# GpSimd's order in the first chunk of a recommendation tower: layer 1's low parts before chunk 3's gathers, and twelve idle-time matmuls instead of fourteen

## The chip, the cores and the metric

The kernel runs on one core of a Trainium2 chip. The metric is device time in microseconds (us). Times of runs and of the profiled execution are given apart, since the profile describes one execution alone. PE is TensorE, DVE VectorE, ACT ScalarE, POOL GpSimd, and SP the engine that issues most of the transfers.

## The reference

For each of 512 samples, 39 embedding rows of 16 numbers are gathered from 39 tables. A three-layer compressed interaction network follows, and then a small dense network:

```python
e = stack([tbl_f[ids[:, f]] for f in range(39)], axis=1)        # (512, 39, 16)
x0 = xk = e
for idx, (W, b) in enumerate([(w0, b0), (w1, b1), (w2, b2)]):   # 128 outputs each
    z = relu(einsum('bhd,bkd,hks->bsd', x0, xk, W) + b[None, :, None])
    if idx != 2:
        xk = z[:, :64, :]; direct.append(z[:, 64:, :])
    else:
        direct.append(z)
logit = sum(concatenate(direct, axis=1), axis=-1)               # (512, 256)
h = concatenate([logit, dense_ctx], axis=1)
y = relu(relu(h @ W_top1 + b_top1) @ W_top2 + b_top2) @ W_top3
```

## The kernel before, in words

The batch is cut into 16 chunks of 32 samples, and a chunk's 32 samples times 16 dimensions are the 512 columns of every large operand. For each chunk GpSimd gathers the embedding rows with ten indirect transfers into `emb` (line 360), PE transposes them in two pieces (lines 739 and 744), ACT copies the pieces into `xt`, and SP writes them to the scratch `fields` in memory and loads them back in two layouts: `rep` and `rot` for layer 0 (rotated rows), `bc` for layers 1 and 2 (lines 290, 295, 308 and 315). Even chunks use one buffer of `emb` and `bc`, odd chunks the other.

Each layer then multiplies pairs of rows elementwise on DVE and feeds the products to PE, which sums them over the weights into `z`. The products come in groups of two tiles, of three kinds. A group of kind `w` goes to PE whole, in float32 (DVE line 677, PE line 763). A group of kind `v` or `g` is split: ACT makes the high part (line 496), the low part is raw minus high, and PE runs three matmuls for each tile (lines 753 to 755). For kind `v` DVE computes the low part (line 645), for kind `g` GpSimd does (line 371, `low_g`). Layers 1 and 2 have three `g` groups each, called here the first, second and third low part of a layer and chunk, and a half tile whose low part GpSimd makes partly, too (`stack`, line 365). In layer 1 PE takes the groups in the order 0, 2, 1, 3, 4, 5, 6, 9, 7, 8, where 3, 6 and 8 are of kind `g`; in layer 2 it takes the groups 1, 0, 2, 4, 3, 5 and then 8, 9, 7, 6, where 2, 5 and 6 are of kind `g`.

Every engine runs its own list, in the order written, and semaphores hold the engines together. PE, DVE and ACT go through the layers and chunks in this order: layer 0 of chunk 0, layer 1 of chunk 0, layer 0 of chunk 1, layer 2 of chunk 0, layer 0 of chunk 2, layer 1 of chunk 1, and then three steps for each later phase. GpSimd's list is written out by hand: 30 gathers of chunks 0 to 2, and then chunk 3's ten gathers mixed with the low parts of layers 1 and 2 of chunk 0. A low part waits for its high part, a gather of chunk 3 for the transposes of chunk 1. DVE has two raw slots for `g` products, so its third product of a layer waits for GpSimd's first low part; ACT's high part of the third waits until PE has used the first. When layer 1's last matmul on `z` is done, ACT writes `xk`, with which DVE can begin layer 2 of the chunk.

Ahead of layer 0 of chunk 0, PE has nothing to do until the first products are there, and `keep_busy` runs `FIRST_ROWS` matmuls whose result nobody reads (line 776). A matmul in float32 shows as two rows in the profile.

Of the kernel before, what the change touches and what calls it, by code (L numbers as in the profile page):

```python
# [13 lines left out]
GATHERS = -(-FIELDS // BY)  # L14
# [38 lines left out]
SECTIONS = T1 // SECTION  # L53
STORES = 2 * BY
FOLDS = 3
FIRST_ROWS, FIRST_KEPT = 14, 2
H1, H2, DENSE = 512, 256, 16

DENSE_AT = (0, 32, 64)
# [20 lines left out]
def tower(nc, A, fields, out):  # L80
# [4 lines left out]
    with ExitStack() as ctx:  # L85
# [259 lines left out]
        def _(pool):  # L345
# [9 lines left out]
            def gather(c, columns=range(GATHERS)):  # L355
                if c >= 2:
                    pool.wait_ge(transposed, 2 * (c - 1))
                for j in columns:
                    landed = gathered_first if c == 0 and j < PART // DIM else gathered[c % 2]
                    pool.indirect_dma_start(emb[c % 2][:, j * DIM:(j + 1) * DIM], None, A["tables"],  # L360
                                            bass.IndirectOffsetOnAxis(rows_all[:, c, j:j + 1], 0)).then_inc(landed, 16)
# [5 lines left out]
            def low_part(layer, c, i):  # L367

                k, m = NO["g"][layer, c, groups_of(layer, "g")[i]], ROWS[layer]
                pool.wait_ge(high_ready["g"], k + 1)  # L370
                pool.tensor_tensor(low["g"][0:m, k % PART_SLOTS["g"]], raw[0:m, k % RAW_SLOTS], high["g"][0:m, k % PART_SLOTS["g"]], ALU.subtract).then_inc(low_ready["g"], 1)  # L371
# [20 lines left out]

            for c in range(3):
                gather(c)
            gather(3, range(0, 4))
            low_part(1, 0, 0)
            gather(3, range(4, 6))
            low_part(1, 0, 1)
            stack_part(1, 0)
            low_part(1, 0, 2)  # L400
            gather(3, range(6, 8))
            low_part(2, 0, 0)
            gather(3, range(8, GATHERS))
            low_part(2, 0, 1)
            low_part(2, 0, 2)
            fold01(0)
# [494 lines left out]
```

## Time and profile before

| | us |
|---|---|
| median of 3 runs | 637.71 (637.43 to 641.0) |
| profiled execution, its time | 639.57 |
| profiled execution, its span | 637.2 |
| mean granted clock of TensorE, as a share | 0.995 |

The span runs from the first to the last instruction of the profiled execution; 2.37 us of that execution's time lie around it. The times in rows are counted from the span's start. PE is busy for 606.0 us of the span (95%), DVE for 567.8 (89%), POOL for 485.0 (76%) and ACT for 331.1 (52%).

### The profile page before, as it was taken

The numbers are of one execution on the slowest core, as the hardware profiler recorded it, in microseconds if no ns is written. First come the engines' busy times: TensorE is split into PE (matmuls) and PEld (weight loads), VectorE is DVE, ScalarE is ACT, GpSimd is POOL, SyncE is SP. The second block draws the span as 40 slices with busy tenths as digits, with TensorE's granted clock in tenths as the row PEclk, the third lists the DMA queues.
The fourth block names the chain that finished last, engine by engine and source line by source line (L and its number), as shares of the span: only waits on it lengthen the run. The fifth ranks groups of instructions, "written<-read, shape, count | busy, mean of one in ns | idle before, by whom it ended". The sixth has DMA issues, their size and how long they took to land.

```text
span 637.2 us, 6536 instructions
## 1 busy us (share of the span) xinstructions
PE 606.0 (95%) x2044; PEld 379.8 (60%) x2044; DVE 567.8 (89%) x534; ACT 331.1 (52%) x411; POOL 485.0 (76%) x424
## 2 busy tenths in 40 slices
PE   0896999999999999999999999999999999999998
PEld 0344656565666566666666566666656665756563
DVE  0368799999999999999999999999999999989850
ACT  1323636554747464655646464655547473645432
POOL 6878568987888888888888888888888664565740
PEclk9997999999999999999999999999999999999999
DMA  9799579793948577693939585785939494350200
GB/s 197 179 314 343 177 218 347 217 362 72 351 104 296 177 244 239 180 310 97 366 66 346 132 285 184 224 267 157 332 74 343 101 314 147 129 200 1 72 1 0
DMA packets 126048, 130.13 MB, mean 204 GB/s; under 512 B 60990, under 2 KB 67662, under 8 KB 126015
## 3 DMA queue, kind: packets, MB, share of 16 engines
q1 hardware_dynamic: 117391, 128.27, 63.1%
q0 software_dynamic: 5120, 1.32, 2.0%
q10 hardware_dynamic: 3504, 0.14, 0.4%
q8 instruction: 16, 0.26, 0.2%
q14 instruction: 17, 0.14, 0.1%
HBM read 123.31 MB, written 6.39 MB: 204 GB/s over the span
## 4 chain that ended last, share of the span: by engine, by line
PE 81%; POOL 9%; DVE 5%; issue 3%; DMA 1%; ACT 1%; ACTq 0%; DVEq 0%
PE z L763 35%; PE z L753 14%; PE z L755 13%; PE z L754 13%; POOL emb L360 7%; POOL low_g L371 2%; DVE whole L677 2%; DVE low_v L645 1%; PE z L841 1%; PE z L770 1%; PE z L771 1%; DVE raw L670 1%; DVE raw_bank L664 1%; DMA emb<-in_tables,ids_all 1%; PE raw_bank L831 1%
## 5 line engine op out<-in xcount | busy, mean ns | idle before, releaser
L371 POOL TENSOR_TENSOR low_g<-raw,high_g 128x1024 fp32r<-128x1024 f32 x96 | 229.2, 2390 | 72.8 <-ACT high_g L496 72.4
L763 PE MATMUL z<-whole,w 128*128 128x512 f32 (+2 forms) x608 | 282.1, 593 | 1.8 <-DVE whole L677 1.0
L360 POOL DMA_INDIRECT emb<-in_tables,ids_all x160 | 157.6, 985 | 35.6 <-issue 28.2
L763 PEld LDWEIGHTS z<-whole,w 128*128 128x128 f32 (+2 forms) x608 | 112.9, 189 | 99.9 <-issue 84.4
L496 ACT ACTIVATE high_v<-raw_bank 128x1024 fp32r<-128x1024 f32 (+1 forms) x112 | 114.6, 1023 | 92.8 <-DVE raw_bank L664 92.0
L677 DVE TENSOR_TENSOR whole<-bc,xk 128x1024 f32<-128x1024 f32 (+1 forms) x128 | 137.9, 1078 | 7.9 <-ACT xk L507 5.4
L496 ACT ACTIVATE high_g<-raw 128x1024 fp32r<-128x1024 f32 x96 | 101.5, 1057 | 78.6 <-DVE raw L670 60.1
L645 DVE TENSOR_TENSOR low_v<-raw_bank,high_v 128x1024 fp32r<-128x1024 f32 (+1 forms) x112 | 136.2, 1216 | 3.8 <-ACT high_v L496 3.8
L753 PE MATMUL z<-high_v,w_high 128*128 128x512 f32 (+1 forms) x224 | 126.3, 564 | 1.3 <-DVE low_v L645 1.3
L664 DVE TENSOR_TENSOR raw_bank<-bc,xk 128x1024 f32<-128x1024 f32 x96 | 117.6, 1225 | 7.4 <-ACT xk L507 4.6
L670 DVE TENSOR_TENSOR raw<-bc,xk 128x1024 f32<-128x1024 f32 x96 | 116.3, 1212 | 0.5 <-POOL low_g L371 0.5
L753 PE MATMUL z<-high_g,w_high 128*128 128x512 f32 x192 | 82.6, 430 | 7.2 <-POOL low_g L371 7.1
L755 PE MATMUL z<-low_v,w_high 128*128 128x512 f32 (+1 forms) x224 | 88.0, 393 | 0.0
L754 PE MATMUL z<-high_v,w_low 128*128 128x512 f32 (+1 forms) x224 | 87.6, 391 | 0.0
L755 PE MATMUL z<-low_g,w_high 128*128 128x512 f32 x192 | 75.8, 395 | 0.0
L754 PE MATMUL z<-high_g,w_low 128*128 128x512 f32 x192 | 75.4, 393 | 0.0
L753 PEld LDWEIGHTS z<-high_v,w_high 128*128 128x128 f32 (+1 forms) x224 | 42.4, 189 | 31.4 <-issue 22.3
L754 PEld LDWEIGHTS z<-high_v,w_low 128*128 128x128 f32 (+1 forms) x224 | 42.4, 189 | 27.9 <-issue 22.3
L507 ACT ACTIVATE xk<-z,bias 64x512 f32<-64x512 f32 x64 | 41.6, 650 | 31.5 <-DVE whole L677 17.8
L753 PEld LDWEIGHTS z<-high_g,w_high 128*128 128x128 f32 x192 | 36.3, 189 | 20.6 <-POOL low_g L371 10.1
L755 PEld LDWEIGHTS z<-low_v,w_high 128*128 128x128 f32 (+1 forms) x224 | 42.2, 188 | 9.8
L677 DVE TENSOR_TENSOR whole<-rot,left 120x1024 f32<-120x1024 f32 (+1 forms) x45 | 45.2, 1031 | 0.0
(70 smaller groups left out, 407.3 us busy)
## 6 DMA issues: line engine op xcount, KB each, us to landing
bc<-fields SPq DMA_DIRECT2D x64, 1024.0 KB, 7.3
rot<-fields SPq DMA_DIRECT2D x32, 512.0 KB, 4.8
rot<-fields SPq DMA_DIRECT2D x16, 768.0 KB, 7.0
bc<-fields SPq DMA_DIRECT2D x16, 768.0 KB, 5.2
fields<-xt SPq DMA_DIRECT2D x64, 80.0 KB
bc<-fields SPq DMA_DIRECT2D x32, 128.0 KB, 6.1
rep<-fields SPq DMA_DIRECT2D x48, 80.0 KB
emb<-in_tables,ids_all POOLq DMA_INDIRECT x160, 4.9
```

The costliest lines, as they stand in the source:

```text
L360: pool.indirect_dma_start(emb[c % 2][:, j * DIM:(j + 1) * DIM], None, A["tables"], bass.IndirectOffsetOnAxis(rows_all[:, c, j:j + 1], 0)). ...
L371: pool.tensor_tensor(low["g"][0:m, k % PART_SLOTS["g"]], raw[0:m, k % RAW_SLOTS], high["g"][0:m, k % PART_SLOTS["g"]], ALU.subtract).then_ ...
L496: act.activation(high[kind][0:m, k % slots], src, ACT.Copy).then_inc(high_ready[kind], 1)
L507: act.activation(xk[layer][half * KEEP:(half + 1) * KEEP, :], z[layer][0:KEEP, :], RELU, bias=bias[0:KEEP, layer:layer + 1]).then_inc(x_re ...
L645: nc.vector.tensor_tensor(low["v"][0:m, k % slots], raw_bank[0:m], high["v"][0:m, k % slots], ALU.subtract).then_inc(low_ready["v"], 1)
L664: nc.vector.tensor_tensor(raw_bank[0:m], left, right, ALU.mult).then_inc(raw_ready["v"], 1)
L670: nc.vector.tensor_tensor(raw[0:m, k % RAW_SLOTS], left, right, ALU.mult).then_inc(raw_ready["g"], 1)
L677: nc.vector.tensor_tensor(whole[0:rows, n % WHOLE_SLOTS, 0:len(tiles)], left, right, ALU.mult).then_inc(whole_ready, 1)
L753: nc.tensor.matmul(out_z, w_high[0:m, n, :], high[kind][0:m, k % slots, u], start=first, stop=False)
L754: nc.tensor.matmul(out_z, w_low[0:m, n, :], high[kind][0:m, k % slots, u], start=False, stop=False)
L755: ins = nc.tensor.matmul(out_z, w_high[0:m, n, :], low[kind][0:m, k % slots, u], start=False, stop=False)
L763: ins = nc.tensor.matmul(z[layer][:, :], w[layer][0:m, WHOLE_AT[layer, t], :], whole[0:m, k % WHOLE_SLOTS, u], start=(t == GT * TAKEN[laye ...
```

## The change

GpSimd issues none of chunk 3's gathers ahead of the first low part of layer 1 of chunk 0, two between the first and the second, and the other eight behind the third. Layer 2's three low parts of chunk 0 then follow without gathers between them. PE runs twelve matmuls of `keep_busy` in place of fourteen.

```diff
-FIRST_ROWS, FIRST_KEPT = 14, 2
+FIRST_ROWS, FIRST_KEPT = 12, 2
...
             for c in range(3):
                 gather(c)
-            gather(3, range(0, 4))
             low_part(1, 0, 0)
-            gather(3, range(4, 6))
+            gather(3, range(0, 2))
             low_part(1, 0, 1)
             stack_part(1, 0)
             low_part(1, 0, 2)
-            gather(3, range(6, 8))
+            gather(3, range(2, GATHERS))
             low_part(2, 0, 0)
-            gather(3, range(8, GATHERS))
             low_part(2, 0, 1)
             low_part(2, 0, 2)
             fold01(0)
```

On POOL, from its first gather on, this stood in a row (`emb<-in_tables,ids_all` is a gather with its count behind the x, `low_g` a low part, `stack` the half tile's):

```order
L360 DMA emb<-in_tables,ids_all 128x16 x34
L371 TENSOR_TENSOR low_g<-raw,high_g 128x1024
L360 DMA emb<-in_tables,ids_all 128x16 x2
L371 TENSOR_TENSOR low_g<-raw,high_g 128x1024
L365 TENSOR_TENSOR stack<-stack_raw,stack 64x512
L371 TENSOR_TENSOR low_g<-raw,high_g 128x1024
L360 DMA emb<-in_tables,ids_all 128x16 x2
L371 TENSOR_TENSOR low_g<-raw,high_g 128x1024
L360 DMA emb<-in_tables,ids_all 128x16 x2
L371 TENSOR_TENSOR low_g<-raw,high_g 128x1024 x2
```

At the same place on POOL, this stands now:

```order
L360 DMA emb<-in_tables,ids_all 128x16 x30
L371 TENSOR_TENSOR low_g<-raw,high_g 128x1024
L360 DMA emb<-in_tables,ids_all 128x16 x2
L371 TENSOR_TENSOR low_g<-raw,high_g 128x1024
L365 TENSOR_TENSOR stack<-stack_raw,stack 64x512
L371 TENSOR_TENSOR low_g<-raw,high_g 128x1024
L360 DMA emb<-in_tables,ids_all 128x16 x8
L371 TENSOR_TENSOR low_g<-raw,high_g 128x1024 x3
```

The first low part moved ahead of four gathers, and the fourth, layer 2's first, now has all forty gathers of four chunks before it, as against thirty-eight.

On PE, between the transposes of chunk 0 and the first products of layer 0, this stood before:

```order
L739 MATMUL z<-ident,emb 128x128
L744 MATMUL z<-ident,emb 32x128
L776 MATMUL z<-w,ident 128x512 x14
L763 MATMUL z<-whole,w 128x512 x2
L753 MATMUL z<-high_v,w_high 128x512
```

And this stands there now (the lines of the file have moved up by two):

```order
L737 MATMUL z<-ident,emb 128x128
L742 MATMUL z<-ident,emb 32x128
L774 MATMUL z<-w,ident 128x512 x12
L761 MATMUL z<-whole,w 128x512 x2
L751 MATMUL z<-high_v,w_high 128x512
```

Two of the matmuls with `ident` are gone, and nothing else moved on PE.

## Rows read from the trace of the kernel before

**Rows 1.** The page's chain of work that ended last, by engine.
```profile
PE 81%; POOL 9%; DVE 5%; issue 3%; DMA 1%; ACT 1%; ACTq 0%; DVEq 0%
```

**Rows 2.** Stretches: us, busy time (instructions) per engine, clock, DMA share, GB/s.
```profile
106.00:125.00 19.00, 18.71 (x62) 11.49 (x63) 18.46 (x18) 9.98 (x13) 17.22 (x18) 1.00 0.84 251
...
200.00:300.00 100.00, 100.00 (x345) 63.83 (x343) 99.13 (x94) 56.30 (x70) 85.13 (x76) 1.00 0.68 215
```

**Rows 3.** Timeline of PE, end of keep_busy: start, us, what.
```profile
31.64 2.31 PE L776 MATMUL z<-w,ident 128*128 128x512 f32 x5
...
33.79 1.88 PE L763 MATMUL z<-whole,w 120*128 120x512 f32 x4
```

**Rows 4.** Timeline of DVE, ahead of and in layer 0 of chunk 0.
```profile
24.23 3.62 DVE L634 TENSOR_TENSOR w_low<-bc,w_high 128x3328 fp32r<-128x3328 f32 x1 [12.13 <-ACT w_high L550]
...
31.38 1.23 DVE L677 TENSOR_TENSOR whole<-rot,rep 120x1024 f32<-120x1024 f32 x1 [0.45 <-DMA rot<-fields]
```

**Rows 5.** Timeline of POOL: gathers and low parts; brackets hold idle time before.
```profile
24.45 4.21 POOL L360 DMA_INDIRECT emb<-in_tables,ids_all  x1 [0.30 <-issue]
...
45.45 0.94 POOL L360 DMA_INDIRECT emb<-in_tables,ids_all  x1 [0.30 <-issue]
...
50.44 0.94 POOL L360 DMA_INDIRECT emb<-in_tables,ids_all  x1 [0.30 <-issue]
51.41 2.36 POOL L371 TENSOR_TENSOR low_g<-raw,high_g 128x1024 fp32r<-128x1024 f32 x1
...
56.16 2.41 POOL L371 TENSOR_TENSOR low_g<-raw,high_g 128x1024 fp32r<-128x1024 f32 x1
...
59.75 2.39 POOL L371 TENSOR_TENSOR low_g<-raw,high_g 128x1024 fp32r<-128x1024 f32 x1
62.30 0.96 POOL L360 DMA_INDIRECT emb<-in_tables,ids_all  x1 [0.16 <-issue]
...
71.65 2.39 POOL L371 TENSOR_TENSOR low_g<-raw,high_g 128x1024 fp32r<-128x1024 f32 x1 [7.14 <-ACT high_g L496]
```

**Rows 6.** Timeline of PE, from layer 1 of chunk 0 to chunk 4's transposes.
```profile
53.82 0.79 PE L753 MATMUL z<-high_g,w_high 128*128 128x512 f32 x1 [5.34 <-POOL low_g L371]
...
59.58 0.80 PE L753 MATMUL z<-high_g,w_high 128*128 128x512 f32 x1
...
63.61 0.39 PE L753 MATMUL z<-high_g,w_high 128*128 128x512 f32 x1
...
65.21 0.39 PE L771 MATMUL z<-stack,w_low 128*128 128x512 f32 x1
...
74.44 0.39 PE L753 MATMUL z<-high_g,w_high 128*128 128x512 f32 x1
...
106.03 0.51 PE L753 MATMUL z<-high_g,w_high 128*128 128x512 f32 x1 [0.83 <-POOL low_g L371]
...
114.11 0.33 PE L739 MATMUL z<-ident,emb 128*128 128x128 f32 x1 [0.26 <-DMA emb<-in_tables,ids_all]
```

**Rows 7.** Timeline of ACT and DVE around layers 1 and 2 of chunk 0.
```profile
45.67 1.06 ACT L496 ACTIVATE high_g<-raw 128x1024 fp32r<-128x1024 f32 x1 [1.23 <-DVE raw L670]
...
53.87 1.22 DVE L670 TENSOR_TENSOR raw<-bc,xk 128x1024 f32<-128x1024 f32 x1 [0.53 <-POOL low_g L371]
...
67.00 1.23 DVE L664 TENSOR_TENSOR raw_bank<-bc,xk 128x1024 f32<-128x1024 f32 x1 [3.22 <-ACT xk L507]
```

**Rows 8.** Stretches around PE's long wait; columns as in rows 2.
```profile
50.20:50.40 0.20, 0.00 (x0) 0.00 (x0) 0.20 (x2) 0.01 (x1) 0.00 (x0) 1.00 1.11 374
50.40:50.60 0.20, 0.00 (x0) 0.00 (x0) 0.20 (x1) 0.20 (x1) 0.16 (x1) 0.52 1.06 392
...
57.00:58.00 1.00, 1.00 (x5) 0.86 (x4) 0.00 (x0) 0.98 (x2) 1.00 (x1) 0.88 1.10 397
```

**Rows 9.** Issues of `rot` for chunk 1, second and third, and their landing.
```profile
L295 SPq DMA_DIRECT2D rot<-fields x2: 464/466/469, 50.3 to 50.8; - x2
...
DMA to landing us min/median/max: 6.3/7.1/7.9
```

## The prediction, made before the changed kernel ran

> **What bounds the kernel now.** The chain of waits, read first, ends on PE for 81% of the span and on POOL for 9% [rows 1]. A look at stretches says where which of them holds: from 200 to 300 us PE has no idle time at all and runs at the full granted clock [rows 2], so whatever PE gains ahead of that reaches the end, unless something later gives it back. So I looked for PE's idle time in the first 125 us. The largest is in layer 1 of chunk 0: PE waits 5.34 us, until 53.82, for POOL's first low part [rows 6]. That low part starts at 51.41 [rows 5], though its high part was ready at 45.67 + 1.06 = 46.73 [rows 7]: POOL was still issuing gathers. The last of its 34 gathers starts at 50.44, and the thirtieth ends at 45.45 + 0.94 = 46.39 [rows 5]. The wait also has a second price. TensorE's granted clock falls from 1.00 to about half (2.4 to 1.2 GHz) at 50.4, while PE stands still, and is back only within the stretch from 57 to 58 [rows 8], so the first matmuls after the wait run slowly. Two smaller waits of PE follow, 0.83 us at 106.03 and 0.26 us at 114.11, both at work that POOL delivers [rows 6].
>
> **The low parts of layer 1.** Four gathers leave the place ahead of the first low part. From the thirtieth to the thirty-fourth gather it is 50.44 - 45.45 = 4.99 us, 1.25 each [rows 5]. POOL runs without a wait there, so the first low part starts at 51.41 - 5.0 = 46.4, if its high part is there. Before, that was ready at 46.73; the second edit (below) brings it to 45.6. Behind it POOL's list is the same as before up to the third low part (two gathers, low, stack, low), so I shift the rows by 5.0: the second low part goes from 56.16 to 51.2, the third from 59.75 to 54.75, and its end from 62.14 to 57.1 [rows 5].
>
> PE gets its first g group at 48.8 rather than 53.82. The second low part ends at about 53.6. From PE's second g group to its third, 63.61 - 59.58 = 4.0 us pass [rows 6], at the full clock, so the third group comes at 57.6 at the latest, when its low part is 0.5 us old. From there to the end of layer 1 it is 65.21 + 0.23 - 63.61 = 1.83 us (0.23 is the distance of such matmuls at the full clock: 65.21 - 63.61 over seven). Layer 1 of chunk 0 ends at 59.4 instead of 65.44, **6.0 to 6.1 us earlier**: the five of POOL, and about one that PE and DVE lost otherwise (the slow matmuls; and DVE's third raw product, which waited 0.53 us for the same low part [rows 7]). DVE was idle for 3.22 us up to 67.00 for exactly this end [rows 7], by way of ACT, so it starts layer 2 at about 61.
>
> **The eight gathers.** They now stand between layer 1's third low part and layer 2's first. POOL's first gather behind the third low part moves from 62.30 to 57.3 [rows 5]; seven more at 1.25 and the length of one end at 57.3 + 8.75 + 0.95 = 67.0. Layer 2's first low part, from 71.65, could with DVE's new times start at 65.5, so the gathers now hold it up: it goes from 67.05 to 69.4. Before, POOL stood idle for 7.14 us at this place [rows 5], which pays for the gathers. PE, which took that low part at 74.44 [rows 6], gets it at 69.45, **5.0 earlier**, and waits about 1.2 us for it: a new wait, POOL's again. The two low parts behind it have lost the gathers that stood between, so with high parts 6.1 us earlier POOL is 6.1 ahead from the third of them on. Chunk 3's embeddings, whose last gather starts at 66 instead of 75, are not late for anyone.
>
> **The two smaller waits.** With DVE and POOL 6.1 us ahead and PE only 5.0, the wait of 0.83 at 106.03 goes, and that at 114.11 shrinks with it: POOL's order behind layer 2 is unchanged, and chunk 4's last gather is also 6.1 earlier. PE ends up 5.0 + 0.83 + 0.26 = **6.1 us earlier** past 114, where DVE's and POOL's 6.1 are the next limit. Behind that PE is full and keeps it.
>
> **Two matmuls of keep_busy fewer.** The last rows of keep_busy are (33.79 - 31.64) / 5 = 0.43 us apart [rows 3]. Two matmuls are four rows, 1.72 us; PE would be through at 32.07. DVE's first whole product ends at 31.38 + 1.23 = 32.61 [rows 4], so PE starts at 32.65 and 1.14 of the 1.72 is saved; what hid it is gone, DVE is what comes last there. Layer 0 of chunk 0, ACT's `xk` and DVE's products of layer 1 are all 1.14 us earlier. At the end of the kernel it is not added to the 5.0, since POOL's gathers from 3.88 us on don't depend on it: it only sees to it that high parts are ready before POOL wants them. By itself it would be worth 0 to 1.1 us, in this sum 0.3 (46.73 against 46.4).
>
> **What is unknown.** The third part of chunk 1's `rot` is issued at 50.8 and lands 7.9 us later, at 58.7 [rows 9]. DVE's layer 0 of chunk 1 will want it at about 57.4 (the third raw product at 52.2, then four instructions of at most 1.22 each). If SP's chain moves by the same 1.14 us, it lands at 57.6 and nothing is lost; if the transfer engines are so full that it doesn't move (shares of 1.06 to 1.11 in that stretch [rows 8]; these are means that can exceed one), DVE loses 1.3, of which 0.5 is free ahead of layer 2, so 0.8. I take 0.2, nearer to the first, because SP waits there for ACT. A gain below nothing is excluded, since nobody waits for it earlier than this.
>
> **The sum.** 6.1 - 0.2 = 5.9 us. The profiled span would be 631.3, its time 639.57 - 5.9 = 633.7. The profiled execution lies 1.86 above the median of the runs; against the median it is 637.71 - 5.9 = **631.8**. A measurement of this kernel tells about 1% (6.4 us) from no change, and the forecast lies just inside it.
>
> **Rival: the clock falls all the same.** The gap of 5.34 becomes one of 53.82 - 48.8 = 5.0 less, plus the 1.1 by which PE is there earlier, so some 1.5 us; then PE waits briefly again for the second low part. Before, the clock fell about 2 us into PE's wait [rows 6, 8], which speaks against it, but between 47 and 54 PE is still idle for over a quarter of the time (1.5, then some 0.4 ahead of the next two groups). Then some fourteen matmuls cost 0.2 us more each (0.43 for 0.23), 2.8, of which the gaps absorb 1 or more: the end is 1 to 2 us worse, 632.8 to 633.8. Such a delay reaches the end in full, since it also takes from DVE's and POOL's 6.1.
>
> **Rival: the eight gathers are held up, and the kernel gets slower.** One gather took 4.21 us instead of 0.94, from 24.45 [rows 5], just while DVE ran a long subtraction with both inputs in SBUF, from 24.23 to 27.85 [rows 4]. If the eight gathers met such work, each would cost up to 3.3 more, 26 us in all, and layer 2's first low part would start at 93 instead of 71.65. Slower than before begins at 5.0 us of delay, two gathers blocked. What speaks against it: between 57 and 67 DVE's products take one factor from a PSUM bank, and the gathers from 45.45 to 50.44, beside such products, all kept 0.94. Blocked for four gathers of the eight, it is 8 us slower: 646.
> The Trainium skill says the same of the cause (SBUF — State Buffer, Who interferes with whom): a VectorE instruction with two SBUF inputs contends with a GpSimd instruction that reads SBUF, and the one that comes second blocks fully, while one SBUF input does not contend. By that rule the eight gathers run free, as in the sum; the trace agrees at 4.21 us.
>
> **Rival: the gain is given back.** If chunk 4's embeddings or DVE were the real limit of the stretch up to 125, where DVE is busy for 18.46 of 19.00 us [rows 2], and they didn't move, PE would wait for them and the end stay where it is, at 637. Against it: DVE's wait at 67.00 is for PE's layer 1, which does move, and POOL's idle 7.14 us shows that POOL can.
>
> **How the numbers follow.** Forecast 0.72, with its own range from 631.0 to 632.7 (gains of 6.7 to 5.0: POOL's part alone at the one end, 0.6 of luck with transfers and matmuls at the other). The clock 0.14, given back 0.07, gathers held up 0.04, and 0.03 for a larger gain. The range from 630.9 to 633.9 takes in the forecast and the clock and leaves out the rest. Faster by over 1% needs 6.4 us, which the upper edge of the forecast and the larger gain reach: 0.29. Slower by over 1% is the blocked gathers: 0.03. Within 1%: 0.68.
>
> **What would show it.** POOL's first low part starts at 46.4 and PE's wait ahead of it is 1.5 instead of 5.34; the clock stays at 1.00 through 50 to 58; layer 1 of chunk 0 ends at 59.4; POOL's eight gathers run from 57.3 to 67.0 at 1.25 each; PE waits about 1.2 us for layer 2's first low part, at 69.45; the waits at 106.03 and 114.11 are smaller or gone. The prediction is wrong if DVE starts layer 2 later than 62, if a gather of the eight is much longer than 0.94, or if PE's steady part does not start 5 to 6 us earlier.

## The result, and the profile after

| | before | changed |
|---|---|---|
| median of 5 runs | 637.85 | 635.36 |
| lowest to highest | 637.43 to 641.0 | 634.74 to 635.69 |
| profiled execution, its time | 639.57 | 634.74 |
| profiled execution, its span | 637.2 | 632.4 |

The ratio of the runs is 0.9949, with a 95% interval from 0.9929 to 0.9968. The change is faster, clear of the noise, but by 2.5 us between the medians, where 5.9 were forecast. The two profiled executions are 4.83 us apart, much nearer to the forecast than the medians: the later sections are about this difference.

POOL's timeline in the changed kernel, which answers to rows 5:

```profile
45.00 0.94 POOL L360 DMA_INDIRECT emb<-in_tables,ids_all  x1 [0.30 <-issue]
46.95 2.38 POOL L371 TENSOR_TENSOR low_g<-raw,high_g 128x1024 fp32r<-128x1024 f32 x1 [1.00 <-ACT high_g L494]
...
51.70 2.41 POOL L371 TENSOR_TENSOR low_g<-raw,high_g 128x1024 fp32r<-128x1024 f32 x1
54.55 1.29 POOL L365 TENSOR_TENSOR stack<-stack_raw,stack 64x512 fp32r<-64x512 f32 x1 [0.44 <-ACT stack L501]
55.81 2.38 POOL L371 TENSOR_TENSOR low_g<-raw,high_g 128x1024 fp32r<-128x1024 f32 x1
58.34 0.96 POOL L360 DMA_INDIRECT emb<-in_tables,ids_all  x1 [0.16 <-issue]
...
67.09 0.94 POOL L360 DMA_INDIRECT emb<-in_tables,ids_all  x1 [0.30 <-issue]
68.05 2.40 POOL L371 TENSOR_TENSOR low_g<-raw,high_g 128x1024 fp32r<-128x1024 f32 x1
```

The first low part starts at 46.95 instead of 51.41 [rows 5], and now it is POOL that waits, 1.00 us, for ACT's high part. The eight gathers run unhindered from 58.34 to 68.03, and layer 2's first low part comes right behind them, in the place where POOL stood idle for 7.14 us before [rows 5].

PE's timeline, which answers to rows 6 (the second piece of the same engine is its start of layer 0, as in rows 3):

```profile
49.39 0.51 PE L751 MATMUL z<-high_g,w_high 128*128 128x512 f32 x1 [0.77 <-POOL low_g L371]
51.69 0.51 PE L751 MATMUL z<-high_v,w_high 128*128 128x512 f32 x1 [0.64 <-DVE low_v L643]
...
60.34 0.39 PE L769 MATMUL z<-stack,w_low 128*128 128x512 f32 x1
70.51 0.51 PE L751 MATMUL z<-high_g,w_high 128*128 128x512 f32 x1 [0.76 <-POOL low_g L371]
109.28 0.33 PE L737 MATMUL z<-ident,emb 128*128 128x128 f32 x1 [0.22 <-DMA emb<-in_tables,ids_all]
```

```profile
20.69 13.40 PE L774 MATMUL z<-w,ident 128*128 128x512 f32 x24 [0.36 <-ACT xt L478]
33.93 1.88 PE L761 MATMUL z<-whole,w 120*128 120x512 f32 x4
```

PE's wait of 5.34 us is down to 0.77, layer 1 of chunk 0 ends at 60.6 instead of 65.4, and the transposes of chunk 4 start at 109.28 instead of 114.11, 4.83 earlier, which is the whole difference of the two executions. But layer 0 starts at 33.93, where before it started at 33.79 [rows 3], although keep_busy has four rows fewer: its 24 rows took 13.4 us, 0.56 each, because the first of them ran slowly for longer. The granted clock is listed as 1.00 there in both profiles, so what these rows show is the distance of the rows, and not a clock.

DVE's timeline between the two, around the end of chunk 1's layer 0 and the start of chunk 0's layer 2 (67.00 before [rows 7]):

```profile
59.10 1.22 DVE L675 TENSOR_TENSOR whole<-rot,left 120x1024 f32<-120x1024 f32 x1 [0.37 <-DMA rot<-fields]
...
62.13 1.23 DVE L662 TENSOR_TENSOR raw_bank<-bc,xk 128x1024 f32<-128x1024 f32 x1
```

Stretches as in rows 8 and 2: the clock stays at 1.00 through the place where it fell before, and the steady part is as full as it was.

```profile
50.40:50.60 0.20, 0.20 (x2) 0.17 (x1) 0.20 (x2) 0.07 (x1) 0.04 (x1) 1.00 1.05 410
57.00:58.00 1.00, 1.00 (x5) 0.68 (x4) 1.00 (x2) 0.36 (x1) 1.00 (x1) 1.00 1.05 391
200.00:300.00 100.00, 100.00 (x346) 64.18 (x345) 99.10 (x95) 56.77 (x72) 85.05 (x76) 1.00 0.70 214
```

### The profile page after: what moved, and what is told of

Same layout as the page of the kernel before. It is cut to its first block, busy times and chain, and to the rows that moved or that the text cites. A ratio compares the mean times of both kernels' runs of the same rounds, so it can differ in the third digit from the quotient of the medians.

```text
span 632.4 us, 6528 instructions
## 1 busy us (share of the span) xinstructions
PE 604.9 (96%) x2040; PEld 378.5 (60%) x2040; DVE 568.1 (90%) x534; ACT 331.1 (52%) x411; POOL 484.8 (77%) x424
## 3 DMA queue, kind: packets, MB, share of 16 engines
HBM read 123.31 MB, written 6.39 MB: 205 GB/s over the span
## 4 chain that ended last, share of the span: by engine, by line
PE 84%; DVE 6%; POOL 4%; issue 2%; DMA 2%; ACT 1%; ACTq 0%; DVEq 0%
PE z L761 36%; PE z L751 14%; PE z L753 14%; PE z L752 13%; POOL emb L360 2%; PE z L774 2%; DVE whole L675 2%; DVE low_v L643 2%; DMA emb<-in_tables,ids_all 2%; POOL low_g L371 2%; DVE raw L668 1%; DVE raw_bank L662 1%; PE z L839 1%; PE z L768 1%; PE z L769 1%
```

## The experiments

Each is compared with runs of the kernel before on the same chip in the same hour. The medians of those lie between 637.85 and 639.40, so the ratios are compared, and not the times, which the expectations name. For the changed kernel the ratios were 0.9949 and, in a second set, 0.9953. Profiled executions can be compared directly, across chips too: in all sixteen, from the start of chunk 4's transposes (109.28 to 114.11 us) to the end of the execution's time it is 525.42 to 525.48 us. So whatever sets them apart has happened before that point.

**The new order on POOL alone, and the two matmuls alone.**

```diff
 # e1: the changed kernel
-FIRST_ROWS, FIRST_KEPT = 12, 2
+FIRST_ROWS, FIRST_KEPT = 14, 2
 # e2: the kernel before
-FIRST_ROWS, FIRST_KEPT = 14, 2
+FIRST_ROWS, FIRST_KEPT = 12, 2
```

> The new order on POOL with the old fourteen matmuls of keep_busy. Theory 1: the order brings the gain, and in the new order layer 0's end reaches the end of the kernel; how long keep_busy takes depends on when TensorE's clock rises in an execution (23.1 us in the profile of before, 26.7 in that of the changed kernel), and two matmuls more cost 0 to 1.7 us: a median of 635.4 to 637.0, best guess 636.2, that is 0 to 1.7 us over the changed kernel. Rival: the two matmuls are worth nothing or did harm: 635.4 or less.

> The old order on POOL with twelve matmuls of keep_busy. Theory 1: the first low part still starts behind 34 gathers at about 51.4, whatever layer 0 does, so the median stays at that of before, 637.4 to 638.2. Rival: an earlier layer 0 reaches the end by another way (DVE): 636.5 to 637.0.

The order alone: 636.23 (634.87 to 636.97), ratio 0.9964 (0.9950 to 0.9978). The two matmuls alone: 638.73 (637.51 to 640.36) beside 638.42, ratio 1.0002 (0.9990 to 1.0015). So the gain is the order's, and in the old order the two matmuls are worth nothing. The changed kernel's ratios (0.9949 and 0.9953) would put the two matmuls at 0.7 to 1.0 us in the new order, as theory 1 says, but the intervals overlap, and e5 and e6 below speak against it. What e1's expectation calls the rise of the clock, at 23.1 and 26.7 us, is the moment at which keep_busy's rows come closer together.

**The kernel before, twice more.** Nothing is edited in e4 and e11; they show how one execution differs from the next.

> The kernel before, once more, for a second profile and for the width of its times. Theory 1: another execution shows the clock fall and rise at other moments around PE's wait, its time lies nearer to 637.8 than the first profile's 639.57, and the ratio is 1.000 within 0.002. Rival: the fall lies at 50.4 and the rise near 57.4 again, with about the same eight slow matmuls, and the 1.7 us between the first profile and the median lie elsewhere.

> The kernel before, a third profile. Theory: its time goes with two things that differ between executions, the start of POOL's first low part (51.41 at 639.57, 50.54 at 639.31) and the time for which the clock stays at half behind PE's wait (6.83 us in both): an execution near 637.8 shows the low part at 49.5 to 50.5 or a half clock of about 3.4 us. Rival: an execution near 637.8 shows neither.

The runs of the kernel before beside e4 lie between 636.37 and 640.5 (31 runs, median 638.42), and e4's own median is 638.51, ratio 1.0003 (0.9989 to 1.0017). The profile of e4 (639.31) is like the first: PE waits 4.10 us, and the clock is at half until past 57, though it fell 0.7 us later than in the first. So it does not decide between theory 1 and the rival. In the profile of e2 (637.51) PE waits 3.83 us, and the clock is back by 56. PE's timeline and a stretch of e4, and PE's timeline and two stretches of e2:

```profile
52.95 0.79 PE L753 MATMUL z<-high_g,w_high 128*128 128x512 f32 x1 [4.10 <-POOL low_g L371]
```

```profile
57.00:58.00 1.00, 1.00 (x4) 0.81 (x3) 0.31 (x1) 0.64 (x2) 1.00 (x2) 0.55 1.01 356
```

```profile
51.88 0.50 PE L753 MATMUL z<-high_g,w_high 128*128 128x512 f32 x1 [3.83 <-POOL low_g L371]
```

```profile
55.00:56.00 1.00, 1.00 (x4) 0.76 (x4) 1.00 (x2) 0.86 (x1) 1.00 (x1) 0.65 1.04 391
56.00:57.00 1.00, 1.00 (x5) 0.61 (x4) 0.98 (x3) 0.80 (x2) 1.00 (x2) 1.00 1.07 393
```

The profile of e11 (636.60) differs more. POOL's and PE's timelines and a stretch of e11:

```profile
25.20 3.87 POOL L360 DMA_INDIRECT emb<-in_tables,ids_all  x1 [0.31 <-issue]
...
49.56 2.38 POOL L371 TENSOR_TENSOR low_g<-raw,high_g 128x1024 fp32r<-128x1024 f32 x1
```

```profile
35.61 0.59 PE L763 MATMUL z<-whole,w 120*128 120x512 f32 x1
...
51.99 0.50 PE L753 MATMUL z<-high_g,w_high 128*128 128x512 f32 x1 [1.70 <-POOL low_g L371]
```

```profile
52.00:53.00 1.00, 1.00 (x4) 0.85 (x5) 1.00 (x2) 0.79 (x1) 0.90 (x1) 1.00 1.10 334
```

In this execution of the unchanged kernel POOL's first low part starts at 49.56 instead of 51.41 [rows 5]; keep_busy ended late, so layer 0 started at 35.61 instead of 33.79 [rows 3], and PE's wait is 1.70 instead of 5.34 [rows 6]; the clock does not fall at all. It is 2.97 us faster than the first profiled execution, and its chunk 4 transposes start 2.97 us earlier (111.14). The wait that the prediction read from rows 6 is the longest of the four. The execution near 637.8 that the expectation asked for is e2's: its low part starts at 49.45, and its clock is at half for 3.4 us.

How often the clock falls can be counted without profiles, since each run's mean granted clock is on record. It is 0.995 in the first profile and in e4 (6.8 us at half), 0.997 in e2 (3.4 us) and 1.000 in e11. The 77 runs of the kernel before that stand beside the experiments have 0.995 in 32, 0.997 in 40 and 1.000 in 5, and their times go with it:

| mean clock | runs | median, us |
|---|---|---|
| 0.995 | 32 | 639.53 |
| 0.997 | 40 | 638.17 |
| 1.000 | 5 | 636.99 |

So the clock falls in nearly every run of the old order, a run like e11 is rare, and the first profiled execution belongs to the slower of the two common groups. The sets differ in the share of these groups: 3 of 17 runs have 0.995 in the set with the median 638.26, and 9 of 14 in that with 639.40. All eleven runs of the changed kernel have 1.000.

The start of the low part moves because the 34 gathers ahead of it take more or less time: one of them meets DVE's long subtraction and takes 4.21 us [rows 5], 3.31 in e4, 3.50 in e2, and one to three later ones meet DVE's first products. Over the 34 gathers, the time beyond 0.94 each is 5.4 us in the first profile, 4.7 in e4, 3.6 in e11 and 3.5 in e2, and the low parts start at 51.41, 50.54, 49.56 and 49.45.

**PE's wait filled.** Five matmuls that nobody reads, into a bank that is idle there, ahead of layer 1's first g group of chunk 0 in the kernel before. e10 is the same kernel a second time.

```diff
                 for g in TAKEN[layer]:
...
                     else:
+                        if (layer, c, g) == (1, 0, 3):
+                            keep_busy(5, xk[1])
                         split_group(layer, c, g)
```

> The kernel before, with five matmuls that nobody reads (into an idle bank) in PE's 5.3 us wait for the first low part. Theory 1: the half clock behind that wait cost the profiled execution of before about 1.6 us (eight matmuls at 0.43 instead of 0.23), the median execution less; filled, the clock stays at 1.00 through 48 to 58, and the median is 636.9 to 637.7 with a smaller spread than before. Rival a: every execution of before pays the 1.6: 636.2. Rival b: the half clock costs nothing at the end: 637.85.

> The kernel with PE's wait filled, once more, for a second profile (its times fall into two groups, near 636.9 and near 638.4). Theory: the clock stays at 1.00 and the time goes with the start of POOL's first low part (50.1 at 636.90): 638.4 would go with a start near 51.5. Rival: in the slower group the clock falls all the same.

The median is 637.94 beside 638.42, ratio 0.9986 (0.9973 to 0.9998). The profile of e3 (636.90), PE's timeline and a stretch:

```profile
48.58 4.45 PE L776 MATMUL xk<-w,ident 128*128 128x512 f32 x10
...
52.54 0.72 PE L753 MATMUL z<-high_g,w_high 128*128 128x512 f32 x1
```

```profile
57.00:58.00 1.00, 1.00 (x5) 0.60 (x4) 1.00 (x1) 0.00 (x0) 1.00 (x2) 1.00 1.00 369
```

One of e3's twelve runs took 3607 us, for a reason that is not known, and is not in the ratio. The clock stays up, in all twelve runs, and the kernel gains a little, 0.1%: theory 1's size, not the 1.6 us that rival a takes from every execution. The second look refutes what was expected of it. At 638.17 its low part starts at 49.62, not near 51.5; the clock is at 1.00, so the rival is out, too. There keep_busy ended at 35.3, where it ended at 34.0 in e3, the filling ran on to 53.76, past the low part's end at 52.0, and held PE up; DVE also waited 1.26 us for the half tile's transfer. The two starts of layer 0 are 1.29 us apart and the two times 1.27; whether that is what makes the two groups of this kernel's times, two profiles don't show.

Since the filling can hold PE up by itself, e3's median prices the slow clock too low. The profiles give the price more directly: from its first g group to the end of layer 1 PE takes 11.62 us in the first profile, 12.29 in e4 and 11.62 in e2, where the clock is at half for a part of it, and 10.36 in e11 and 10.34 in e3 and e10, where it is not. That is 1.3 to 1.9 us (in e2 with a wait of DVE for `bc` in it, 0.98 us).

**What the end follows in the new order.** e5 is the changed kernel again; e6 and e7 have fewer matmuls of keep_busy; e8 moves the last two gathers.

```diff
 # e6, e7: the changed kernel
-FIRST_ROWS, FIRST_KEPT = 12, 2
+FIRST_ROWS, FIRST_KEPT = 10, 2      (e7: 8)
 # e8: the changed kernel
-            gather(3, range(2, GATHERS))
+            gather(3, range(2, 8))
             low_part(2, 0, 0)
+            gather(3, range(8, GATHERS))
```

> The changed kernel once more, for a second profile and as the mark for the three kernels beside it. Its median is 635.0 to 635.8, and the ratio 0.995 within 0.002.

> The changed kernel with ten matmuls of keep_busy in place of twelve. Theory 1: in the new order the end of layer 0 reaches the end of the kernel, until POOL's thirtieth gather (45.9 to 46.4) comes last; keep_busy ended at 33.9 in the profile of the changed kernel, where DVE's product was ready at 32.3, so four rows of 0.43 fewer save up to 1.7 us there and up to 1.0 at the end: 634.6 to 635.0. Rival: keep_busy's length does not reach the end, 635.4 as before the edit.

> The changed kernel with eight matmuls of keep_busy. Theory 1: nothing is left to save beyond ten, since DVE's product at 32.3 comes last: 634.4 to 635.0, the same as with ten. Rival: PE's idle time ahead of layer 0 (up to 3.7 us) lets the clock fall, layer 0 runs at half speed and ends up to 2 us later: 635.8 to 637.

> The changed kernel with the last two of chunk 3's gathers behind layer 2's first low part instead of ahead of it. That low part can start at 66.7 instead of 68.05, and PE's wait of 0.76 us there goes. Theory 1: what is earlier at the end is set by DVE's chain from layer 1's end (4.8 us earlier than in the profile of before), not by this low part, and PE's gain is taken by its waits near 101 and 109: 635.1 to 635.6, no change. Rival: this low part sets the end: 634.5 to 634.8.

| | median | ratio, 95% interval |
|---|---|---|
| e5, as changed | 635.73 | 0.9953 (0.9940 to 0.9967) |
| e6, ten | 635.65 | 0.9956 (0.9944 to 0.9969) |
| e7, eight | 636.48 | 0.9972 (0.9962 to 0.9982) |
| e8, two gathers later | 635.55 | 0.9957 (0.9944 to 0.9969) |

e8 agrees with theory 1. Its profile shows the low part of layer 2 earlier, and PE's wait for it down to 0.16 us, and what PE gained there it waits at the next two places:

```profile
69.86 0.50 PE L752 MATMUL z<-high_g,w_high 128*128 128x512 f32 x1 [0.16 <-POOL low_g L371]
101.95 0.50 PE L752 MATMUL z<-high_g,w_high 128*128 128x512 f32 x1 [0.88 <-POOL low_g L371]
110.08 0.33 PE L738 MATMUL z<-ident,emb 128*128 128x128 f32 x1 [0.34 <-DMA emb<-in_tables,ids_all]
```

e7 agrees with the rival: PE stood idle for 3.22 us ahead of layer 0 and the clock fell in it, so that layer 0 ran at half. It does so in part of the runs only: the mean clock is 0.995 in five of the twelve (median 637.58), 0.997 in four (636.26) and 1.000 in three (635.66).

```profile
33.00 2.04 PE L761 MATMUL z<-whole,w 120*128 120x512 f32 x2 [3.22 <-DVE whole L675]
```

```profile
34.00:36.00 2.00, 2.00 (x5) 0.97 (x3) 1.88 (x3) 0.00 (x0) 1.70 (x2) 0.50 1.06 379
```

e6 refutes theory 1 on its own ground. Layer 0 did start earlier, at 32.60 instead of 33.93, and yet nothing came of it. PE's, DVE's and SP's timelines in e6:

```profile
32.60 1.96 PE L761 MATMUL z<-whole,w 120*128 120x512 f32 x4 [0.95 <-DVE whole L675]
...
60.69 0.39 PE L769 MATMUL z<-stack,w_low 128*128 128x512 f32 x1
```

```profile
53.14 0.69 DVE L697 TENSOR_TENSOR stack_raw<-bc,xk 128x512 f32<-128x512 f32 x1 [1.49 <-DMA bc<-fields]
```

```profile
41.07 6.39 SPq L256 DMA_DIRECT2D fields<-xt  x8
47.50 0.43 SPq L308 DMA_DIRECT2D bc<-fields  x1
47.98 1.15 SPq L315 DMA_DIRECT2D bc<-fields  x2
```

DVE waits 1.49 us for the transfers of `bc` at the half tile, a wait that is not there in the first profile of either kernel. SP begins chunk 1's stores 1.1 us earlier than before, but issuing the eight takes 6.39 us while the transfers of `bc` ahead of them are still running, and the last part of `bc` is issued at 47.5 and 48.0. An earlier layer 0 does not bring this issue forward: in the first profiles of both kernels, e1, e2, e4, e5, e6 and e8 layer 0 starts between 32.60 (e6) and 34.44 (e1), and the issue stands between 46.89 and 47.95, at 47.50 in e6 and at 47.12 in e1. e5 has the same wait at 0.88 us; e1 and e8 don't have it, and wait for the third part of chunk 1's `rot` instead, 1.04 and 1.24 us. What e6 still has in hand at the start of layer 2 (62.48, where e5 has 62.96) it gives back to the next transfer, chunk 2's `rot`:

```profile
80.29 1.22 DVE L675 TENSOR_TENSOR whole<-rot,left 120x1024 f32<-120x1024 f32 x1 [0.56 <-DMA rot<-fields]
```

In the end chunk 4's transposes start at 110.17 in e1, 110.12 in e5 and 110.19 in e6, with fourteen, twelve and ten matmuls and layer 0 1.84 us apart. So theory 1 became theory 2: the transfers between 42 and 60 us hold DVE's chain.

**The transfers.** e9 (with ten matmuls) loads the half tiles ahead of chunk 1's stores; e13 (twelve) and e14 (ten) load all of chunk 0's `bc` ahead of them.

```diff
 # e9: half_tiles is the loop over half of load_broadcasts, a function of its own, left out there for c = 0
             load_broadcasts(0, range(SECTIONS - 1))
+            half_tiles(0)
             store_issue(1)
             load_broadcasts(0, range(SECTIONS - 1, SECTIONS))
 # e13, e14
-            load_broadcasts(0, range(SECTIONS - 1))
+            load_broadcasts(0)
             store_issue(1)
-            load_broadcasts(0, range(SECTIONS - 1, SECTIONS))
```

> The changed kernel with ten matmuls of keep_busy, and chunk 0's two half tiles loaded ahead of chunk 1's stores instead of behind them. With ten matmuls DVE waited 1.49 us for the half tile at 53.14. Theory 2: the transfers between 42 and 60 now set DVE's chain, and the next one stands right behind: the third part of chunk 1's rot lands at about 59.2, so DVE ends layer 0 of chunk 1 at 62.1, where it now begins layer 2 of chunk 0 at 62.3; DVE's wait moves from the half tile to rot, and the median is 635.3 to 635.7. Rival: the half tile alone held the chain: 634.2 to 634.7.

> The changed kernel with all of chunk 0's bc, the last section and the half tiles too, loaded ahead of chunk 1's stores. Theory 2: the wait of DVE for the half tile near 53 goes, but the stores and with them chunk 1's rot come behind one more megabyte (about 2.7 us at some 370 GB/s), so its third part lands between 59 and 61 and takes over: 635.3 to 636.3. Rival: the half tile was the only limit left: 634.5 to 635.0.

> The same order of transfers with ten matmuls of keep_busy, so that layer 0 ends up to 1 us earlier. Theory 2: chunk 1's rot holds DVE at the same moment, so the two matmuls are worth nothing: within 0.4 us of the kernel with twelve. Rival: with the half tile out of the way the earlier layer 0 reaches the end: 633.8 to 634.5.

e9: 636.05 beside 638.87, ratio 0.9964 (0.9951 to 0.9976). That is no better than e6, so the rival did not come, but for theory 2 it tells little: DVE's wait at the half tile counts the last section of `bc`, too, which was not moved, and is still there at 0.46 us. e13: 637.26, ratio 0.9971 (0.9958 to 0.9983); e14: 637.40, ratio 0.9971 (0.9959 to 0.9982), both beside 639.40. DVE's timeline of e14:

```profile
58.07 1.23 DVE L661 TENSOR_TENSOR raw_bank<-rot,left 120x1024 f32<-120x1024 f32 x1 [2.76 <-DMA rot<-fields]
...
61.41 1.22 DVE L674 TENSOR_TENSOR whole<-rot,left 120x1024 f32<-120x1024 f32 x1 [0.81 <-DMA rot<-fields]
```

The wait at the half tile is gone, and `rot` of chunk 1 has taken its place with 3.57 us in two pieces; in e13 they are 2.55 and 0.81, at the same moments, 58.08 and 61.42, although its layer 0 starts 0.3 later. That is theory 2; it undersized the price, since the ratio is worse than the changed kernel's and not equal to it. The stores took 9.49 us to issue in e13 and 9.88 in e14, instead of 4.82 in the first profile of the changed kernel. The rivals of both did not come.

**Half of the move.**

```diff
+            gather(3, range(0, 2))
             low_part(1, 0, 0)
-            gather(3, range(0, 2))
+            gather(3, range(2, 4))
             low_part(1, 0, 1)
...
-            gather(3, range(2, GATHERS))
+            gather(3, range(4, GATHERS))
```

> The changed kernel with two of chunk 3's gathers ahead of layer 1's first low part, two behind it, and six behind the third low part: half of the move. Theory 2: in typical executions of the old order the first low part starts at 49.5 to 50.5, and its high part is ready at about 46.9, so only 2.6 to 3.6 of the 5.0 us moved can count; two gathers fewer ahead (2.5 us) bring nearly all of it, 636.0 to 636.5. Rival: the gain goes with the gathers moved, half of it is left: 636.9 to 637.2.

636.61 beside 639.40, ratio 0.9958 (0.9943 to 0.9974), with half the gathers moved: as much as the full move brought, and not the 0.9975 of half of it, which lies at the interval's edge. The set beside it is the slowest one, which flatters the ratio. In its profile the low part starts at 48.97 and PE waits 3.44 us, in an execution with a long row of gathers (one of 4.38). The rival isn't far enough off to be called refuted by this one experiment.

## Why the prediction was wrong

**The mechanism was right, and its parts are in the trace.** POOL's gathers held up the first low part, and moved they don't; the clock's fall behind PE's wait is gone; the eight gathers took 9.7 us, mostly where POOL was idle, and none was blocked; PE has the new wait for layer 2's first low part (0.76 us, at 70.51, said to be 1.2 at 69.45); the wait at 106.03 is gone and that at 114.11 is 0.22. The rivals of the clock and of the blocked gathers did not come. The steady part took the gain to the end, 4.83 us at 109.28 and at the end.

**The step that failed is the sum's last: "against the median it is 637.71 - 5.9".** The text saw that the profiled execution lay 1.86 us above the median of its runs, and put the whole gain on the median all the same. But the gain was worked out from a wait of 5.34 us and eight slow matmuls, and an execution without these is not as slow. e4, e2 and e11 show the same old order with waits of 4.10, 3.83 and 1.70 us, and a clock that is at half until 57.9, until 55.7, or not at all; their times are 639.31, 637.51 and 636.60. The mean clock of the runs says the same: the first profiled execution is one of the group at 0.995, and the typical run at 0.997 takes 1.4 us less. Forecast and measurement are 3.4 us apart: between the two profiled executions 4.83 of the 5.9 came, so 1.1 went in the changed kernel, and the other 2.3 lie in which executions were profiled: 639.57 is 1.72 over its median of five runs, 634.74 is 0.62 under its own, and lacks the wait for `bc` that e5's profile of the same kernel (635.60) has.

**The gain itself came out 1.1 us short.** In the prediction's sum PE is 5.0 us earlier at layer 2's first low part, and 0.83 + 0.26 come on top. Measured, that is 74.44 - 70.51 = 3.93, then 0.83 and 0.04: 4.80 of the 6.1, of which the prediction kept 5.9. The prediction's own signs show it, too: DVE starts layer 2 at 62.13, and it was to be wrong if that came later than 62. Two terms stand behind that, the next two.

**"1.14 of the 1.72 saved" came to nothing.** The term took the length of keep_busy from one execution, in which its rows came 0.43 us apart from about 23.5 us on. In the changed kernel's profile they were slow (some 0.85 apart) until about 26.7, and layer 0 started 0.14 later instead of 1.14 earlier. POOL's first low part then waited for ACT until 46.95, layer 1 ended at 60.6 instead of 59.4, and DVE's and POOL's 6.1 became 4.8. And e6 shows that the 1.1 would not have come through with faster rows: there layer 0 did start 1.19 earlier than in rows 3, and the end was no earlier than in the changed kernel.

**"I take 0.2" was the wrong end.** The prediction bounded one transfer, `rot` of chunk 1, and argued that SP's chain would move with ACT. It does not move: SP's stores stand behind `bc`'s transfers, whose time is not tied to layer 0 (e6: begun 1.1 us earlier, and done no earlier). In the changed kernel's profile DVE waits 0.37 us for this `rot`, and 0.62 to 1.24 in e1, e5, e8 and e9. Another transfer of the same chain, the last of `bc`, holds DVE before that in e5 and e6, with up to 1.5 us; the prediction did not name it. With it gone, `rot` is next, and holds DVE at the same moment whether layer 0 ends earlier or later (e13, e14).

**What stays open.** How long the old order's wait is was seen in four executions (and two filled ones); the mean clock tells of every run whether the clock fell, but not how long PE waited. How the 1.1 us divide between the late start of layer 0 and the transfers was not measured in the changed kernel's own execution. And why the first rows of keep_busy are slow for longer in one execution than in another is not shown.

## What to carry to other kernels

A gain that is read from a wait in one profiled execution belongs to that execution: if it lies above the median of the runs, look first at whether the wait, or the slow clock behind it, is what put it there. A second profile, and the mean clock of each run, show that at little cost; take the gain against a typical execution, and not against the one at hand. Close behind a wait that is removed there can be another: here transfers that are issued in order did not come earlier when the work that allows them did. Before a head start is counted, find the transfers it needs and what they queue behind.

## What the runs showed of the hardware that was not expected

The moment at which TensorE's first matmuls double their pace differs between executions of the same matmuls, while the granted clock is listed as 1.00 throughout. The first row of keep_busy starts at 20.3 to 20.6 us in the first profile, e1, e4 and e11, and layer 0 behind 28 rows starts at 33.79 [rows 3], 34.16 in e4, 34.44 in e1 and 35.61 in e11: 1.8 us between executions, from work that nobody reads.

An indirect gather on GpSimd that meets DVE's subtraction of 3.6 us (both inputs in SBUF) took 4.21 us [rows 5], 3.31 in e4 and 3.87 in e11, against 0.94 for most others, and the whole row of gathers ends up to 2 us earlier or later for it. In all sixteen profiles this gather ends 0.81 to 0.83 us after the subtraction does, wherever it began (3.22 to 4.38 us long), as if nearly all of its 0.94 came behind it. DVE's timeline of e11, for the gather at 25.20 above, which ends at 29.07:

```profile
24.62 3.63 DVE L634 TENSOR_TENSOR w_low<-bc,w_high 128x3328 fp32r<-128x3328 f32 x1 [12.20 <-ACT w_high L550]
```

The later ones that were longer than 0.94 do the same: in the first profile a gather runs from 32.05 to 33.42, and the product of two SBUF operands that it meets ends at 32.61 [rows 4]. So how long the row of gathers is depends on where each of them stands against DVE's instructions of this kind.

Eight stores that SP issues behind running transfers took 4.14 us to issue in e11, where they began at 43.99, 4.67 in the first profile (42.18), 6.39 in e6 (41.07) and 9.49 in e13 with one more megabyte ahead of them.
